# Last expert layer in two passes, the second over tokens sorted by group, with gate products taken in halves

## The reference, cut to what matters

```python
flat = (flat - mu) * rsqrt(var + LN_EPS) * ln_scale + ln_bias
h_shared = _swiglu(flat @ shared_in_w.T)
out_shared = h_shared @ shared_out_w.T + shared_out_b
g_idx = argmax(flat @ group_gate_w.T + group_bias, -1)
e_sel = take_along_axis((flat @ expert_gate_w.T).reshape(S, G, EG), g_idx[:, None, None], axis=1)[:, 0, :]
e_probs = softmax(e_sel + expert_bias.reshape(G, EG)[g_idx])
topv, topi = top_k(e_probs, 2);  topv = topv / (topv.sum(-1, keepdims=True) + 1e-08)
h_expert = _swiglu(flat @ expert_in_w.T)
for e in range(8):
    routed = routed + comb[:, e:e + 1] * (h_expert @ expert_out_weight[e].T)
return out_shared + (cnt @ expert_out_bias + routed)
```

## Time and profile before

| what | value |
|---|---|
| median of three runs | 1778.42 us |
| the profiled execution's own time | 1775.86 us |
| its span, first to last instruction | 1773.9 us |
| PE busy, PEld busy | 1388.5 us, 992.5 us |
| DVE, ACT, POOL busy | 1134.5, 677.5, 800.8 us |
| normalization block of the last layer | about 1345 to 1393 us |
| `mix_experts` | about 1393 us to the end |

### The profile page before, as it was taken

The page is one execution under the profiler, slowest core; times in us unless marked ns, Lnnn a source line. Parts: engine busy times, 40 slices in busy tenths (PEclk is TensorE's granted clock), DMA queues, the critical chain, the costliest instruction groups (busy, mean ns, idle before and its releaser), DMA issues. The chain is left out here.

```text
span 1773.9 us, 27554 instructions
## 1 busy us (share of the span) xinstructions
PE 1388.5 (78%) x9068; PEld 992.5 (56%) x9068; DVE 1134.5 (64%) x1837; ACT 677.5 (38%) x1150; POOL 800.8 (45%) x833
## 2 busy tenths in 40 slices
PE   5679999999873332876727848888998699999998
PEld 3567777777542221765625623333334478887877
DVE  2755555555367782211114888888885889888998
ACT  3234444444443321322203548787875311111111
POOL 1455445444320034888865237777743333232331
PEclk9889999999985565999867969999999899999999
DMA  4070000000001032544443000000001000000000
GB/s 168 1 289 15 0 0 0 0 0 0 0 1 26 1 102 64 100 78 86 78 106 128 1 2 2 1 0 0 0 1 40 1 9 13 13 13 13 9 13 17
DMA packets 56803, 61.75 MB, mean 35 GB/s; under 512 B 15507, under 2 KB 46577, under 8 KB 55425
## 3 DMA queue, kind: packets, MB, share of 16 engines
q1 hardware_dynamic: 40835, 49.69, 8.6%
q0 software_dynamic: 13888, 10.24, 4.2%
q10 hardware_dynamic: 2016, 1.00, 0.2%
HBM read 36.49 MB, written 25.59 MB: 35 GB/s over the span
## 5 line engine op out<-in xcount | busy, mean ns | idle before, releaser
L1946 PE MATMUL at_slot<-at_qm,at_ks 128*128 128x512 bf16 (+1 forms) x640 | 160.3, 384 | 19.5 <-DVE at_clip L2151 10.2
L502 PE MATMUL ga_kv<-ga_kern,ga_v 128*128 128x274 f32 x512 | 133.5, 403 | 13.5 <-ACT ga_kern L591 12.6
L2667 DVE TENSOR_REDUCE mx_routed<-mx_weighted 128x128 f32<-128x1024 f32 x69 | 138.1, 2001 | 2.4
L2625 POOL TENSOR_TENSOR mx_h_E<-mx_hid_E,mx_h_E 128x768 fp32r<-128x768 f32 x23 | 43.5, 1890 | 188.8 <-DVE mx_h_E L2657 188.8
L84 PE MATMUL mx_e<-ff_expert_out_high,mx_h_E 128*128 128x512 f32 x276 | 112.3, 407 | 10.7 <-DVE mx_weighted L2664 10.7
L2030 ACT ACTIVATE at_clip<-at_slot,at_four 128x1024 bf16<-128x1024 f32 (+1 forms) x96 | 106.9, 1113 | 32.1 <-PE at_slot L1946 30.3
L1429 POOL DMA_INDIRECT moe_sums<-ex_y,slot_sums x69 | 108.4, 1570 | 22.4 <-issue 20.3
L2151 DVE TENSOR_SCALAR at_clip<-at_slot 128x1024 bf16<-128x1024 f32 (+1 forms) x96 | 116.1, 1218 | 3.1 <-PE at_slot L1946 2.8
L502 PEld LDWEIGHTS ga_kv<-ga_kern,ga_v 128*128 128x128 f32 x512 | 92.2, 189 | 37.8 <-ACT ga_kern L591 16.8
L85 PE MATMUL mx_e<-ff_expert_out_low,mx_h_E 128*128 128x512 f32 x276 | 109.6, 397 | 0.0
L653 POOL TENSOR_TENSOR ga_rot<-ga_by_cos,ga_by_sin 128x274 f32<-128x274 f32 x64 | 48.6, 759 | 134.9 <-DVE ga_by_sin L697 134.9
(11 more groups left out here) (457 smaller groups left out, 3835.9 us busy)
## 6 DMA issues: line engine op xcount, KB each, us to landing
moe_sums<-ga_zeros SPq DMA_DIRECT2D x8, 1152.0 KB, 13.4
ar_rows<-moe_sums SPq DMA_DIRECT2D x34, 256.0 KB, 3.9
ex_down<-in_down SPq DMA_DIRECT2D x32, 192.0 KB, 2.5
token_rows<-ct_rows SPq DMA_DIRECT2D x17, 256.0 KB, 2.4
out_h<-H SPq DMA_DIRECT2D x22, 192.0 KB, 1.9
H<-in_text SPq DMA_DIRECT2D x1, 4096.0 KB, 21.4
patches<-in_patches SPq DMA_DIRECT2D x1, 1728.0 KB, 8.2
ga_sin<-in_sin SPq DMA_DIRECT2D x1, 1644.0 KB, 7.9
```

What stands on the lines that cost most here:

```text
L502: last = nc.tensor.matmul(kv[:, e, 0:HALF], v[p][:, mt + 2 * side, e * P:(e + 1) * P], kern[(p + g) % 2][:, side, :], start=mt == 0 and si ...
L1946: last = nc.tensor.matmul(to[r0:r0 + r, g % 2, :].rearrange("p (s n) -> p s n", s=2), ks[m][:, t * P:t * P + r], qm[m][:, 2 * g:2 * g + 2, ...
L2667: nc.vector.tensor_reduce(R[p][t][:], weighted[:].rearrange("p e d -> p d e"), AX.X, ALU.add).then_inc(reduced, 1)
```

## The change

`mix_experts` goes over the tokens twice.

The first pass (23 chunks of 384 tokens in the old order) computes the shared expert and the biases only. Its result `H` is turned to tokens on rows (`turn_rows`), copied (`keep_rows`) and stored into `out_h`, which now has a row for each token.

Beside it, the normalized tokens are turned to rows (`stage_turn`, 69 PE transposes in 18 groups; `keep_stage` on ACT), the four shares and the token's number are put behind each row of 128 values (133 in all), and POOL scatters the 69 tiles into a table `by_group` in memory: tokens of the first group from the front, tokens of the second from the back. Their places come from a prefix count in `rank` on PE and `place_tokens` on DVE. A DMA in `last_norm` first fills the table with a constant blank from an input, 8960 rows.

The second pass takes the table in 70 tiles, four to a chunk of 512, 18 chunks (the last with two tiles): SP loads a chunk, PE turns it (`turn`), `project2` makes the experts' gate products, and `experts` only the four experts of the tile's group, 512 columns picked by a register. ACT weighs the first expert (`weigh_first`), DVE adds the other three (`weigh`, three operations with one share each), and POOL adds the 128 rows into `out_h` with an indirect DMA by token number. Four buffers hold loaded chunks, six hold weighed tiles, both in the space of `F`.

In both passes each gate product is taken in two halves f = 0, 1 (`project`, `swish`, `hide` and the high and low parts of one half each). High parts are made by ACT and low parts by DVE; POOL does no arithmetic in this stage any more. `route` is cut in three: `place_tokens`, `expert_odds` and `choose_experts`, with the halves of `hide` and `hide_low` of chunks 0 and 1 between them. The semaphores of `run_experts` are taken from a list that is cleared after that layer.

```diff
+            sp.dma_start(grouped_d, x["blank"]).then_inc(blanked, 16)
             sp.wait_ge(loaded, 16 * len(weights))
             sp.wait_ge(gates_in, 16)
+            sp.wait_ge(blanked, 16)
...
-def mix_experts(nc, k, H, F, GL, high, low, out):
+def mix_experts(nc, k, x, H, F, GL, high, low, grouped_d, out):
...
+        silu = sb("silu", [P, 2, GCH])
+        hid = sb("hid", [P, 2, GCH])
+        h = [[sb(f"h{p}{q}", [P, 2, GCH], F32R) for q in range(2)] for p in range(2)]
+        f_parts = [[sb(f"f{p}{q}", [P, GCH], F32R) for q in range(2)] for p in range(2)]
...
+        LOADS, RING = 4, 6
+        tiles = [F[:, p * GT * GROW:(p + 1) * GT * GROW].rearrange("p (t d) -> p t d", d=GROW) for p in range(LOADS)]
+        R = [F[:, LOADS * GT * GROW + p * P:LOADS * GT * GROW + (p + 1) * P] for p in range(RING)]
...
+            def load(c):
+                t, n = CHUNKS2[c]
+                if c >= LOADS:
+                    t0, n0 = CHUNKS2[c - LOADS]
+                    for j in range(t0, t0 + n0):
+                        sp.wait_ge(sent[j % RING], 16 * (j // RING) + 16)
+                sp.dma_start(tiles[c % LOADS][:, 0:n, :],
...
-            def experts(c, p, t):
-                if t == 0:
-                    pe.wait_ge(low_done, 2 * c + 1)
-                tokens = slice(t * P, (t + 1) * P)
-                for a in range(2):
-                    pe.wait_ge(weighed, 6 * c + 2 * t + a + 1)
-                    for f in range(2):
-                        cols = slice(a * 512, (a + 1) * 512)
-                        last = split_matmul(nc, e_ps[a][:], [part[:, f, tokens] for part in h["E"][p]],
-                                            (high["expert_out"][:, f, cols], low["expert_out"][:, f, cols]), f == 0, f == 1)
-                    last.then_inc(expert_done, 1)
...
+            def experts(c, i, first_count):
+                j = CHUNKS2[c][0] + i
+                if j == 0:
+                    pe.wait_ge(added, CHUNKS)
+                elif j == 1:
+                    pe.wait_ge(rows_out, CHUNKS)
+                else:
+                    pe.wait_ge(weighed, j - 1)
+                at = (((P * j + BEYOND - first_count) >> BEYOND_BITS) & 1) * 512
...
-                nc.tensor.matmul(y_ps[:, 0:CH], low["out_bias"][:], cnt_t[:], start=False, stop=True)
-                pe.wait_ge(reduced, CT * c + CT)
-                for t in range(CT):
-                    last = nc.tensor.transpose(r_ps[:, t * P:(t + 1) * P], R[p][t][:], k["ident"][:])
-                last.then_inc(y_done, 1)
-
...
-            def body(c, p, first, final):
-                experts(c, p, 0)
-                if not first:
-                    finish(c - 1, 1 - p)
-                if not final:
-                    project(c + 1, 1 - p, "E")
-                experts(c, p, 1)
-                turn_cnt(c)
-                if not final:
-                    project(c + 1, 1 - p, "S")
-                experts(c, p, 2)
-
-            pe.sem_inc(cnt_ps, 1)
-            project(0, 0, "E")
-            project(0, 0, "S")
-            loop(pe, body)
...
+            for c in range(CHUNKS - 1):
+                if c > 0:
+                    project(c + 1, 0)
+                    turn_rows(c - 1)
+                    project(c + 1, 1)
+                turn_cnt(c + 1)
+                finish(c)
+            turn(0)
+            turn_rows(CHUNKS - 2)
+            finish(CHUNKS - 1)
+            first_count = nc.tensor.value_load(boundary[0:1, 0:1], min_val=0, max_val=NT)
+            project2(0, 0)
+            turn(1)
+            turn_rows(CHUNKS - 1)
+            project2(0, 1)
+            for c, (t, n) in enumerate(CHUNKS2):
+                if c < LAST2:
+                    project2(c + 1, 0)
+                if c + 2 <= LAST2:
+                    turn(c + 2)
+                for i in range(n):
+                    experts(c, i, first_count)
+                    if i == min(1, n - 1) and c < LAST2:
+                        project2(c + 1, 1)
 
...
+            def weigh_first(c, i):
+                j = CHUNKS2[c][0] + i
+                act.wait_ge(expert_done, j + 1)
+                if j >= RING:
+                    act.wait_ge(sent[j % RING], 16 * (j // RING))
...
+            for c in range(CHUNKS):
+                keep_cnt(c)
+                if c + 2 < CHUNKS:
+                    tokens_high(c + 2)
+                if c == 1:
+                    keep_rows(0)
+                if 0 < c and c + 1 < CHUNKS:
+                    swish(c + 1, 0)
+                    hide_high(c + 1, 0)
+                    if c > 1:
+                        keep_rows(c - 1)
+                    swish(c + 1, 1)
+                    hide_high(c + 1, 1)
...
+            for c, (t, n) in enumerate(CHUNKS2):
+                if c < LAST2:
+                    swish2(c + 1, 0)
+                if c + 2 <= LAST2:
+                    tokens_high2(c + 2)
+                if c < LAST2:
+                    hide_high2(c + 1, 0)
+                for i in range(n):
+                    weigh_first(c, i)
+                    if i == min(1, n - 1) and c < LAST2:
+                        swish2(c + 1, 1)
+                        hide_high2(c + 1, 1)
...
+            pool.wait_ge(placed_at, 1)
+            pool.wait_ge(combined, 2)
+            for t in range(TILES):
+                if t % 4 == 0:
+                    pool.wait_ge(staged, t // 4 + 1)
+                nc.gpsimd.indirect_dma_start(out=grouped_d, out_offset=bass.IndirectOffsetOnAxis(ap=place_i[:, t:t + 1], axis=0),
+                                             in_=stage[:, t, :], in_offset=None, bounds_check=GTILES * P - 1,
+                                             oob_is_err=False).then_inc(placed, 16)
+            pool.wait_ge(placed, 16 * TILES)
+            pool.sem_inc(grouped, 1)
+            for p in range(2):
+                pool.wait_ge(stored[p], 16 * len(range(p, CHUNKS, 2)) + 16 * (p == (CHUNKS - 1) % 2))
+            for j in range(GTILES):
+                pool.wait_ge(weighed, j + 1)
+                ids = tiles[j // GT % LOADS][:, j % GT, GROW - 1:GROW].bitcast(I32)
+                nc.gpsimd.indirect_dma_start(out=out, out_offset=bass.IndirectOffsetOnAxis(ap=ids, axis=0),
+                                             in_=R[j % RING], in_offset=None, bounds_check=NT - 1, oob_is_err=False,
+                                             compute_op=ALU.add).then_inc(sent[j % RING], 16)
...
-            def weigh(c, p, t):
-                n = 6 * c + 2 * t
-                for a in range(2):
-                    dve.wait_ge(expert_done, n + a + 1)
-                    by = comb[:, bass.ds(CT * c + t, 1), 4 * a:4 * a + 4].rearrange("p o e -> p (o e)").unsqueeze(2).broadcast_to([P, 4, P])
-                    nc.vector.tensor_tensor(weighted[:, 4 * a:4 * a + 4, :], e_ps[a][:].rearrange("p (e d) -> p e d", e=4),
-                                            by, ALU.mult).then_inc(weighed, 1)
-                dve.wait_ge(weighed, n + 4)
-                nc.vector.tensor_reduce(R[p][t][:], weighted[:].rearrange("p e d -> p d e"), AX.X, ALU.add).then_inc(reduced, 1)
-                dve.wait_ge(reduced, CT * c + t + 1)
...
+                nc.vector.tensor_tensor(hc, hc, e_ps[c % 2][:, 0:CH], ALU.add).then_inc(added, 1)
...
+            def weigh(c, i):
+                j = CHUNKS2[c][0] + i
+                r = R[j % RING]
+                share = lambda e: tiles[c % LOADS][:, i, P + e:P + e + 1]
+                part = lambda e: e_ps[j % 2][:, e * P:(e + 1) * P]
+                dve.wait_ge(first_done, j + 1)
+                for e in range(1, 4):
+                    if e > 1:
+                        dve.wait_ge(acc, 2 * j + e - 1)
+                    nc.vector.scalar_tensor_tensor(r, part(e), share(e), r, ALU.mult, ALU.add).then_inc(acc if e < 3 else weighed, 1)
+
...
+            tokens_low(0)
+            tokens_low(1)
+            place_tokens()
+            for f in range(2):
+                hide(0, f)
+            expert_odds()
+            for f in range(2):
+                hide_low(0, f)
+            for f in range(2):
+                hide(1, f)
+            choose_experts()
+            for f in range(2):
+                hide_low(1, f)
...
+            for c in range(CHUNKS):
+                if c > 0:
+                    add(c - 1)
+                if c + 2 < CHUNKS:
+                    tokens_low(c + 2)
+                if 0 < c and c + 1 < CHUNKS:
+                    hide(c + 1, 0)
+                    hide_low(c + 1, 0)
+                    hide(c + 1, 1)
+                    hide_low(c + 1, 1)
...
+            for c, (t, n) in enumerate(CHUNKS2):
+                if c < LAST2:
+                    hide2(c + 1, 0)
+                if c + 2 <= LAST2:
+                    tokens_low2(c + 2)
+                for i in range(n):
+                    weigh(c, i)
+                    if i == 0 and c < LAST2:
+                        hide_low2(c + 1, 0)
```

(3 more changed lines are left out.)

444 lines of the change are left out of this document (294 added, 150 removed).

## The result

On the chip of the first measurement the changed kernel took 1704.82 us (median of 4 runs, 1703.96 to 1705.0) and the kernel before 1778.17 in the same session: ratio 0.9588, 95% interval 0.9572 to 0.9605. Predicted were 1713 (1690 to 1752). The profiled span went from 1773.9 to 1703.1.

What follows compares the result with a forecast made beforehand. Bound by ACT's chain in the first pass, DVE with ACT in the second: 1425 + 109 + 8 + 156, then the tail to 1708, 66 us under the profiled span; against the median 1713 us, range 1690 to 1752.

Steps and rivals of the forecast that it cites:

- Start of the first pass: In mix_experts, the first pass's steady pace was to start near 1425 us, where the old kernel had its own from 1417.
- First pass: Shared expert and biases: 21 chunks at 5.17 us each, 109 us in all; PE's own work 4.5 a chunk.
- ACT's chain sets this pace: First pass: ACT's operations and its waits for DVE take 5.17 us a chunk, against 4.5 on PE.
- Between the passes: Chain from the last finish to the first expert matmul: 10 us, of which 8.4 count before the second pass's pace.
- Second pass: The sorted experts: 17 chunks at 9.2 us each, 156 us in all.
- DVE with ACT sets the pace: Second pass: DVE's 7.9 us plus 1.3 waiting for ACT make 9.2 a chunk, over PE's 8.8.
- better overlap: Rival for both passes: hand-overs cost nothing and PE is the bound, 21 us less, 1692 us; chance 0.12.
- Tail: After the second pass's pace: last two tiles to 1703 us, POOL's last addition and the end to 1708.
- DMAs: Scatter issues 88 us, 1421 to 1511, hidden; adding DMA hidden; second-pass chunk loads hidden with 1 us to spare.
- the scatter is dear: Rival: a scatter issue costs 1.88 us, 130 in all, ending at 1552; total 1735 us; chance 0.08.
- DVE waits for POOL's DMAs: Rival: DVE operations with two SBUF inputs wait for POOL's issues, 19 us first pass, 18 second; 1750 us; chance 0.12.
- The slower side: Rival: small first-pass gaps keep PE at 1.2 of 2.4 GHz, 8.3 us a chunk; 1787 us; chance 0.04.

## Right and wrong, step by step

- *Start of the first pass*, 1425: measured 1429.2, of which 2.4 us arose before the stage (the transposes that end the block before start 2.35 us later than in the kernel before, 1395.51 against 1393.16). That is no effect of the change: with the same code before the stage, four other kernels on this chip start them at 1393.6 to 1397.4. The stage itself needed 1.9 more. The waits were foreseen (`hide_low(0)` until 1414.4, measured 1416.25), but not that they are a price of this order, nor that PE would fall to the low clock in its own 6.6 us wait.
- *First pass*, 21 x 5.17 = 109: measured 104.5 (1429.2 to 1533.7). The step that failed is "ACT's chain sets this pace". ACT's seven operations were priced by their printed durations, 3.5 us, and its two waits for DVE at 1.65. One operation right behind another starts earlier than that: `tokens_high` 0.38 after `keep_cnt` (1487.79 to 1488.17), printed 0.48. ACT was busy 67.54 of 105 us, 3.05 a chunk, and with fewer matmuls its chain came to 3.07 + 1.38 = 4.45 instead of 5.17. PE's own 4.5 was too little: it took 4.74, with two switches of 0.25. PE had been priced by starts, the others by durations, and this made them look like the bound.
- *Between the passes*, 8: measured 8.9 (1533.7 to 1542.6).
- *Second pass*, 17 x 9.2 = 156: measured 152.5. "DVE with ACT sets the pace" was wrong by the same error: DVE busy 121.16 of 153 us makes 7.0 a chunk, not 7.9. With fewer matmuls it was busy 6.9 and idle 1.45, together the 8.34 of that run. PE's 8.8 was right to 0.04. That the sum came within 3.5 us is luck: it named the wrong engine, whose row was taken 0.9 too long, and the right one lay only 0.4 below. The rival *better overlap* had the mechanism; its 1692 took too much from the first pass, whose PE work and switches make 4.74, not 4.5.
- *Tail*: 10 us after the pace, measured 8.0 (1695.1 to 1703.1).
- Together from the last transposes: 314.8 predicted (1708 - 1393.2), 307.6 measured (1703.1 - 1395.5), and 1.9 - 4.5 + 0.9 - 3.5 - 2.0 = -7.2. A late start and two passes priced too long cancel in part, so 1704.8 for 1713 looks better than the account behind it.
- *DMAs*: scatter 88 us, measured 92 (19 of the 69 issues took 1.13 to 1.31), hidden; its price 0.97 + 0.30 was right for the others, so *the scatter is dear* falls. The load did not quite have its 1 us to spare: PE waited for it 8 times, 3.0 us in the whole pass, which the prediction had named as a sign of being wrong; it cost little.

```profile
PEld mx_t L2625 <- DMA ff_tokens<-by_group: 3.0, 8, 0.5
```

- *DVE waits for POOL's DMAs*: falls. `tokens_low` and `hide_low`, two inputs in SBUF, took 0.52 to 0.56 us beside an issue of POOL's (57 of them) and 0.55 to 0.56 alone (12). The Trainium skill (SBUF — State Buffer, section "SBUF: two separate sides") says that such an operation and a GpSimd operation that reads SBUF exclude each other. This trace does not show it for an indirect DMA's issue, 0.52 to 0.56 us beside one. The first two operations of the decision, 1.67 and 0.99 us in the kernel before, took 0.87 and 0.30 with POOL silent.
- *Halved gate products* stand in the prediction's sum but were given no value of their own, so it could not say which part of the change gains: 1.49 us a chunk in the first pass (some 31 us for 21 chunks) and 15 to 18 us in the second. With the 93 us of the sorting they make some 140 us against a gain of 73 in the stage. What takes the rest back is the second trip over the tokens, with its own projections, turned rows and loads; that is argued from the sum and no run separates it.
- *The slower side*: the low clock did not come (0.98 in the first pass). The prediction's argument against it was a little too strong: a slice of the kernel before with PE at 4 tenths had a clock of 6 as well, and not only those with 2 or 3. On the second kind of chip the kernel is slower than before for a reason that no rival held; there the sum missed by 79 us. The sign of the forecast holds for the first kind alone.

## What to carry to other kernels

Price every engine the same way: where operations stand back to back, by the distance of their starts, since printed durations overlap and make ACT and DVE look 10 to 15% fuller than they are. Where engines wait for each other in a ring and lie near balance, the size of an operation is latency, and halving it can be worth more than moving work; a fixed sequence on one engine should run as soon as its input is there, since anything of another engine's put into it imports that engine's queue. And take the time on more than one chip before calling a change faster: here the sign depended on it.
